# Attention with a third key stack buffer, a new order of its opening, and a low part of the keys made by VectorE in each group

## The chip, the cores and the metric

The kernel runs on one core of a Trainium2 chip. The metric is the device time of one execution in microseconds (us); lower is better.

## The reference

One layer of a perceiver: `x` is (4, 128, 512), the context is (4, 2048, 512). Three steps follow each other, each added to `x` and each behind a layer norm of it. Only the first is touched by the change:

```python
x = x + xattn(layernorm(x), ctx, ctx, w_proj, b_proj)      # 16 heads of 32, no mask
#   scores = einsum('bthd,bshd->bhts', q, k) / sqrt(32);  softmax over s;  einsum with v;  @ w_proj.T + b_proj
x = x + gated_scan_block(layernorm(x), ...)
x = x + mixture_of_experts(layernorm(x), ...)              # 8 experts, top 2, 2 shared
```

## The kernel before

**Groups.** The attention is done in 16 groups (4 batches, 4 sets of 4 heads; group j belongs to batch j // 4). A group has 128 queries, 2048 keys and 4 heads of 32 columns. Numbers are split into a high and a low half of 16 bits, so that a product of 16-bit matmuls keeps nearly the precision of 32 bits: the keys `kt` give `kh` (ScalarE, L423, two heads at a time) and `kl = kt - kh` (POOL, L590, one head at a time, 512 columns each). SyncE's queue then copies both into the *key stack* `kstk` (98 rows: high, low, high, and two rows of ones), with heads along the free dimension. Each half of the 2048 keys takes four copies of `kh` and two of `kl`. `kt`, `kh`, `kl`, `kstk` and the values `v` each have two buffers.

**Work of a group.** TensorE makes 16 blocks of 512 scores for the maxima (`max_scores`, L989), in a ring of two PSUM banks; VectorE takes the maximum of each (`take_max`, L699), and four small reductions make the shift (`shift`, L704 to L710). The shift goes in as two more rows of the queries, which are transposed again (L996). Then TensorE makes the scores a second time, transposed and shifted (`scores`, L1009, 8 steps of 256 keys), ScalarE takes the exponent (L458), POOL adds the two tiles of a step (`pair_sum`, L617), and TensorE multiplies by the values (`values`, L1024) and sums the denominators (`denominators`, L1033). VectorE inverts and divides (L716, L720) one group later.

**Order.** It is written out by hand. Group i is a loop over four parts p. The maxima of group i+1 run beside the scores of group i: blocks 4 to 7 in part 0, 8 to 12 in part 1, 13 to 15 in part 2, and then blocks 0 to 3 of group i+2 in part 3. In part 3 TensorE does blocks 0 and 1, the last two value steps of group i, and then, between the first scores of group i+1, blocks 2 and 3. Block 0 of a group waits for the first half of its key stack (`k_rep`), block 8 for the second. ScalarE splits the keys of group i+3 in parts 0 and 1, POOL makes their low parts after its fourth and sixth sum. At the start of group i SyncE's queue loads the keys of i+4 and the values of i+1, then waits for group i's scores to free the stack and fills it for i+2:

```python
        def stack(j, h):
            sp.wait_ge(split_lo, j + 1)
            if j >= 2:
                sp.wait_ge(st_done, HS * (j - 2) + HS // 2 * (h + 1))
            copies(j, h, kh, (0, 2 * HD))
            copies(j, h, kl, (HD,))
```

**Opening.** Before the loop, SyncE's queue loads batch 0 of `x`, the keys of group 0, an identity, rows of ones, the rest of `x`, and the keys of group 1. VectorE normalizes batch 0 (L730), ScalarE makes the high part of two groups' queries (L450), POOL their low part (L602), TensorE transposes them (L977) and ScalarE copies them out (`take_queries`, L435), which in its program stands behind the splitting of group 1's keys. All 16 blocks of group 0's maxima then run alone, then the shift, the first scores and the first blocks of group 1's maxima. VectorE normalizes batches 1 to 3 there.

## Time and profile before

| | |
|---|---|
| runs | 536.14 us median of 3 (534.79 to 537.72) |
| profiled execution | 541.33 us, of it 539.5 us in the span; mean granted clock 0.978 |
| TensorE busy | 471.8 us (87%) |
| VectorE busy | 398.6 us (74%) |
| ScalarE busy | 330.7 us (61%) |
| POOL busy | 293.7 us (54%) |
| maxima by VectorE (L699) | 256 of 686 ns, 163.1 us |
| 16 groups of attention | from about 20 to 294 us of the span |

A row of the timeline or of the chain begins with its start in us of the span and its length in us; "x8" is the number of instructions merged into it. In brackets stands how long the engine was idle before it, and what released it. "issue" stands where no releaser is seen in the records. PE is TensorE, PEld its weight loads, DVE is VectorE, ACT ScalarE, SPq SyncE's DMA queue.

### The profile page before, as it was taken

What the parts mean: (1) busy time and instruction counts of PE and PEld (TensorE: products, weight loads), DVE (VectorE), ACT (ScalarE), POOL (GpSimd) and SP (SyncE); (2) the same over time, 40 slices, a digit from 0 to 9 for tenths busy, and PEclk for the clock granted to TensorE, in tenths of its full rate; (3) what the DMA queues carried; (4) which work ended last, traced back from release to release, by engine and by line L of the source; (5) the groups of instructions that cost most, each with busy time, mean ns of one, the idle gap of its engine ahead of it and who ended that gap; (6) DMA issues with size and microseconds to landing.
All of it is one profiled execution on the core that took longest, in us unless ns stands there. A gap on an engine that the chain in (4) does not pass through costs nothing.

```text
span 539.5 us, 15770 instructions
## 1 busy us (share of the span) xinstructions
PE 471.8 (87%) x6731; PEld 330.4 (61%) x6731; DVE 398.6 (74%) x603; ACT 330.7 (61%) x361; POOL 293.7 (54%) x278
## 2 busy tenths in 40 slices
PE   0478998899997979999999955999999999999995
PEld 0135666666665656676667542854788787887642
DVE  2577776687775767877771799588599999999426
ACT  4245776577675766767555373367478898888320
POOL 2338898999997996999769440373001011010032
PEclk9999999999999998999999996799999999999998
DMA  8598987979979698777698721065999999998125
GB/s 266 110 267 279 254 239 185 230 226 251 258 204 261 157 258 229 230 198 180 139 391 331 293 88 68 1 197 213 421 382 398 417 416 418 416 416 348 40 77 176
DMA packets 48249, 133.94 MB, mean 248 GB/s; under 512 B 6450, under 2 KB 31282, under 8 KB 37426
## 3 DMA queue, kind: packets, MB, share of 16 engines
q1 hardware_dynamic: 44500, 120.88, 69.5%
q0 software_dynamic: 3680, 12.06, 6.1%
q8 instruction: 53, 0.87, 0.7%
q14 instruction: 16, 0.13, 0.1%
HBM read 96.74 MB, written 11.01 MB: 200 GB/s over the span
## 4 chain that ended last, share of the span: by engine, by line
PE 45%; DVE 35%; issue 8%; DMA 6%; POOL 2%; ACT 2%; SPq 1%; DVEq 0%; ACTq 0%; POOLq 0%
DVE mx L699 11%; DVE ws L773 10%; PE bank L1024 8%; PE bank L989 8%; PE bank L1033 7%; PE bank L1009 6%; DMA kt<-in_keysT 4%; DMA wst<-in_ffw 3%; DVE rden L716 2%; PE bank L1147 2%; PE bank L1148 2%; PE bank L1149 2%; DVE hf L914 2%; DVE hl L919 2%; PE bank L1090 1%
## 5 line engine op out<-in xcount | busy, mean ns | idle before, releaser
L699 DVE TENSOR_REDUCE mx<-bank 128x1 f32<-128x512 f32 x256 | 163.1, 686 | 71.2 <-PE bank L989 70.4
L458 ACT ACTIVATE pt<-bank 128x1024 f32<-128x1024 f32 x128 | 125.9, 1023 | 71.1 <-PE bank L1009 71.1
L617 POOL TENSOR_TENSOR ps<-pt 128x512 f32<-128x512 f32 x128 | 160.1, 1280 | 10.9 <-PE bank L1033 5.7
L989 PE MATMUL bank<-kstk,q 96*128 96x512 f16 x256 | 96.9, 410 | 29.2 <-issue 8.7
L773 DVE SCALAR_TENSOR_TENSOR ws<-wst,ws 128x2048 f16<-128x2048 f32 x51 | 115.5, 2287 | 2.0 <-ACT ws L502 1.8
L502 ACT ACTIVATE ws<-wst 128x2048 f16<-128x2048 f32 x48 | 90.5, 1904 | 4.6 <-DMA wst<-in_ffw 4.5
L590 POOL TENSOR_TENSOR kl<-kt,kh 128x512 f16<-128x512 f32 x62 | 70.7, 1166 | 24.9 <-ACT kh L423 24.9
L1009 PEld LDWEIGHTS bank<-q,kstk 98*128 98x128 f16 x1024 | 68.2, 100 | 23.3 <-issue 4.8
L1162 PE MATMUL bank<-xt,ws 128*128 128x128 f16 x480 | 81.2, 219 | 0.8 <-DVE hf L914 0.8
L1009 PE MATMUL bank<-q,kstk 98*128 98x128 f16 x1024 | 80.3, 223 | 1.7 <-ACT pt L458 1.0
L1164 PE MATMUL bank<-xt,ws 128*128 128x128 f16 x480 | 81.2, 219 | 0.0
L1163 PE MATMUL bank<-xt,ws 128*128 128x128 f16 x480 | 81.2, 219 | 0.0
L656 POOL DMA_DIRECT2D ys_rows<-xn x15 | 8.2, 544 | 121.0 <-ACT xn L571 121.0
L1024 PE MATMUL bank<-pt,v 128*32 128x128 f32 x2048 | 69.7, 277 | 0.6 <-issue 0.6
L989 PEld LDWEIGHTS bank<-kstk,q 96*128 96x128 f16 x256 | 22.0, 99 | 62.2 <-DVE mx L699 37.6
L1024 PEld LDWEIGHTS bank<-pt,v 128*32 128x32 f32 x2048 | 58.6, 112 | 1.7 <-issue 1.4
L1162 PEld LDWEIGHTS bank<-xt,ws 128*128 128x128 f16 x480 | 46.9, 98 | 1.2 <-DVE hf L914 1.2
L423 ACT ACTIVATE kh<-kt 128x1024 f16<-128x1024 f32 x32 | 33.4, 1053 | 22.8 <-DMA kt<-in_keysT 22.8
L1163 PEld LDWEIGHTS bank<-xt,ws 128*128 128x128 f16 x480 | 46.9, 98 | 0.0
L1164 PEld LDWEIGHTS bank<-xt,ws 128*128 128x128 f16 x480 | 46.9, 98 | 0.0
L1033 PE MATMUL bank<-ps,ones 128*32 128x128 f32 x1024 | 41.8, 281 | 0.0
L1033 PEld LDWEIGHTS bank<-ps,ones 128*32 128x32 f32 x1024 | 24.7, 110 | 15.4 <-issue 12.2
(162 smaller groups left out, 628.5 us busy)
## 6 DMA issues: line engine op xcount, KB each, us to landing
wst<-in_ffw SPq DMA_DIRECT2D x51, 1024.0 KB, 11.2
kt<-in_keysT SPq DMA_DIRECT2D x16, 1024.0 KB, 6.1
kstk<-kh SPq DMA_DIRECT2D x128, 128.0 KB, 3.4
v<-in_vals SPq DMA_DIRECT2D x16, 1024.0 KB, 9.0
kstk<-kl SPq DMA_DIRECT2D x64, 128.0 KB, 3.8
xs_rows<-biases SPq DMA_DIRECT2D x15, 256.0 KB, 3.0
x_tok<-xs_rows POOLq DMA_DIRECT2D x15, 256.0 KB, 8.4
ys_rows<-xn POOLq DMA_DIRECT2D x15, 256.0 KB, 6.6
```

What stands on the lines that cost most here:

```text
L458: act.activation(pt[:, n % 4, :, :, :].rearrange("p j a t -> p (j a t)"), bank[:, 2 * (n % 2):2 * (n % 2) + 2, :].rearrange("p j n -> p (j ...
L502: act.activation(ws[:, home_of(q), 0, m, :, :].rearrange("p c n -> p (c n)"), wst[:, q % 2, m, :, :].rearrange("p c n -> p (c n)"), ACT.Co ...
L617: pool.tensor_tensor(ps2[:, n % 4, :, :], pt[:, n % 4, 0, :, :], pt[:, n % 4, 1, :, :], ALU.add)\
L699: dve.tensor_reduce(mx[:, a, q:q + 1], bank[:, 4 + k % 2, :], AX.X, ALU.max).then_inc(m_taken, 1)
L773: dve.scalar_tensor_tensor(ws[:, home_of(q), 1, m, :, :].rearrange("p c n -> p (c n)"), wst[:, q % 2, m, :, :].rearrange("p c n -> p (c n) ...
L989: pe.matmul(bank[:, 4 + k % 2, :], q1[:, j % 2, a, :], kstk[0:KS, j % 2, a, q * 512:(q + 1) * 512], start=True, stop=True).then_inc(m_read ...
L1009: mm = pe.matmul(bank[:, 2 * (n % 2) + j, a * P:(a + 1) * P], kstk[:, i % 2, a, tile * P:(tile + 1) * P], q2[:, i % 2, a, :], start=True, ...
L1024: mm = pe.matmul(bank[a * HD:(a + 1) * HD, 6 + i % 2, 0:P], v[:, i % 2, tile, a * HD:(a + 1) * HD], pt[:, n % 4, j, a, :], start=(tile == ...
L1033: mm = pe.matmul(bank[a * HD:(a + 1) * HD, 6 + i % 2, P:2 * P], ones[:, :], ps2[:, n % 4, a, :], start=False, stop=(hs == HS - 1), skip_gr ...
L1162: pe.matmul(o, ws[:, home, 0, m, c, part], xt[:, k % 2, c, :], start=(c == 0), stop=False)
L1163: pe.matmul(o, ws[:, home, 0, m, c, part], xt[:, k % 2, C + c, :], start=False, stop=False)
L1164: mm = pe.matmul(o, ws[:, home, 1, m, c, part], xt[:, k % 2, c, :], start=False, stop=(c == C - 1))
```

## The change

The stack gets a third buffer. It lies in the second half of `wst`, the staging space of the expert weights, which is therefore loaded only after the scores of group 14. In group i the queue now fills the stack of group i+3 instead of i+2: high parts as soon as ScalarE has split, low parts behind the wait for POOL and, new, for VectorE, which makes the low part of the fourth head (`low_of_last`) at the end of part 3 of each group from 0 to 12; POOL makes three heads instead of four. The waits of the key loads follow.

In the opening, the activation tables are loaded early by two small activations; four of the copies for group 0's second half are issued by ScalarE; the queries are copied out before group 1's keys are split; group 0's maxima use six banks and are reduced two banks at a time; group 2's keys are split inside group 0 (ScalarE in parts 0 and 1, VectorE three heads in parts 1 and 2, POOL one) and group 3's there in parts 2 and 3; the first scores go before the first blocks of group 1's maxima; batches 1 to 3 are normalized in groups 1, 5 and 9, in part 1.

```diff
--- before.py
+++ after.py
@@ -141,6 +141,8 @@
     kh = temp("kh", [P, 2, HG, S // 4], F16)
     kl = temp("kl", [P, 2, HG, S // 4], F16)
     kstk = temp("kstk", [KM, 2, HG, S], F16)
+    third = wst[0:KM, 1, :, :, :].rearrange("p m c n -> p (m c n)").bitcast(F16)[:, 0:HG * S]
+    stacks = [kstk[:, 0, :, :], kstk[:, 1, :, :], third.rearrange("p (a s) -> p a s", a=HG)]
     v = temp("v", [P, 2, J, P], F32)
     pt = temp("pt", [P, 4, 2, HG, P], F32)
     ps2 = temp("ps2", [P, 4, HG, P], F32)
@@ -198,13 +200,15 @@
     consts = sem("consts_loaded")
     x_in = sem("x_loaded")
     x0_in = sem("x_first_batch_loaded")
-    id_in = sem("identity_and_ones_loaded")
+    id_in = sem("identity_loaded")
+    ones_in = sem("ones_rows_loaded")
     kt_in = [sem("kt_loaded_0"), sem("kt_loaded_1")]
     v_in = [sem("v_loaded_0"), sem("v_loaded_1")]
-    k_rep = [[sem(f"k_stacked_{q}_{h}") for h in range(2)] for q in range(2)]
+    k_rep = [[sem(f"k_stacked_{q}_{h}") for h in range(2)] for q in range(3)]
     split_hi = sem("split_hi")
     split_lo = sem("split_lo")
     lo_dve = sem("split_lo_by_vector")
+    lo_last = sem("split_lo_of_last_head")
...
@@ -318,11 +322,20 @@
     blk = block.__enter__()
 
 
+    def stack_rows(eng, j, h, src, rows):
+        for row in rows:
+            for q in (2 * h, 2 * h + 1):
+                eng.dma_start(stacks[j % 3][row:row + HD, :, q * S // 4:(q + 1) * S // 4],
+                              src[q * HD:(q + 1) * HD, j % 2, :, :]).then_inc(k_rep[j % 3][h], 16)
+
     @blk.sync
     def _(sp):
         def load_k(j):
             if j >= 2:
                 sp.wait_ge(split_lo, j - 1)
+                sp.wait_ge(lo_dve, 2 * min(j // 2, 2))
+            if j >= 5:
+                sp.wait_ge(lo_last, j - 4)
             sp.dma_start(kt[:, j % 2, :, :], t["keysT"][j]).then_inc(kt_in[j % 2], 16)
 
         def load_v(j):
@@ -331,50 +344,59 @@
             sp.dma_start(v[:, j % 2, :, :], t["vals"][j]).then_inc(v_in[j % 2], 16)
 
         def copies(j, h, src, rows):
-            for row in rows:
-                for q in (2 * h, 2 * h + 1):
-                    sp.dma_start(kstk[row:row + HD, j % 2, :, q * S // 4:(q + 1) * S // 4],
-                                 src[q * HD:(q + 1) * HD, j % 2, :, :]).then_inc(k_rep[j % 2][h], 16)
+            stack_rows(sp, j, h, src, rows)
 
         def stack(j, h):
+            sp.wait_ge(split_hi, 2 * j + 2)
+            if j >= 3:
+                sp.wait_ge(st_done, HS * (j - 3) + HS // 2 * (h + 1))
+            copies(j, h, kh, (0, 2 * HD))
             sp.wait_ge(split_lo, j + 1)
-            if j >= 2:
-                sp.wait_ge(st_done, HS * (j - 2) + HS // 2 * (h + 1))
-            copies(j, h, kh, (0, 2 * HD))
+            if j == 2:
+                sp.wait_ge(lo_dve, 4)
+            if j >= 3:
+                sp.wait_ge(lo_last, j - 2)
             copies(j, h, kl, (HD,))
 
         sp.dma_start(x[:, 0, :], t["x"][:, 0, :]).then_inc(x0_in, 16)
         load_k(0)
         sp.dma_start(idh[:, :], t["idh"]).then_inc(id_in, 16)
-        sp.dma_start(kstk[KS:KM, :, :, :], t["ones"]).then_inc(id_in, 16)
+        sp.dma_start(kstk[KS:KM, :, :, :], t["ones"]).then_inc(ones_in, 16)
+        sp.dma_start(stacks[2][KS:KM, :, :], t["ones"][:, 0, :, :]).then_inc(ones_in, 16)
+        sp.wait_ge(kt_in[0], 16)
         sp.dma_start(x[:, 1:B, :], t["x"][:, 1:B, :]).then_inc(x_in, 16)
-        load_k(1)
         sp.wait_ge(split_hi, 2)
         copies(0, 0, kh, (0, 2 * HD))
-        sp.wait_ge(lo_dve, 1)
+        sp.wait_ge(lo_dve, 2)
         sp.wait_ge(split_lo, 1)
         copies(0, 0, kl, (HD,))
-        stack(0, 1)
+        copies(0, 1, kl, (HD,))
+        load_k(1)
+        load_v(0)
         stack(1, 0)
         load_k(2)
-        load_v(0)
         stack(1, 1)
         load_k(3)
+        load_v(1)
+        stack(2, 0)
+        stack(2, 1)
         for i in range(G):
             if i + 4 < G:
                 load_k(i + 4)
-            if i + 1 < G:
+            if 0 < i < G - 1:
                 load_v(i + 1)
-            if i + 2 < G:
-                stack(i + 2, 0)
-                stack(i + 2, 1)
+            if i + 3 < G:
+                stack(i + 3, 0)
+                stack(i + 3, 1)
             if i == G - 3:
                 for dst, name in CONSTS:
                     sp.dma_start(dst, t[name]).then_inc(consts, 16)
             if i == G - 2:
-                for u in range(2):
-                    for m in range(3):
-                        sp.dma_start(wst[:, u, m, :, :], t["ffw"][2 * u, m]).then_inc(w_in[u][m], 16)
+                for m in range(3):
+                    sp.dma_start(wst[:, 0, m, :, :], t["ffw"][0, m]).then_inc(w_in[0][m], 16)
+        sp.wait_ge(st_done, HS * (G - 1))
+        for m in range(3):
+            sp.dma_start(wst[:, 1, m, :, :], t["ffw"][2, m]).then_inc(w_in[1][m], 16)
 
...
@@ -419,7 +441,7 @@
                 act.wait_ge(kt_in[j % 2], 16 * (j // 2 + 1))
                 if j >= 2:
                     for half in range(2):
-                        act.wait_ge(k_rep[j % 2][half], 16 * 6 * (j // 2))
+                        act.wait_ge(k_rep[(j - 2) % 3][half], 16 * 6 * ((j - 2) // 3 + 1))
             act.activation(kh[:, j % 2, heads, :].rearrange("p a s -> p (a s)"),
                            kt[:, j % 2, heads, :].rearrange("p a s -> p (a s)"), ACT.Copy).then_inc(split_hi, 1)
 
@@ -459,19 +481,21 @@
                            bank[:, 2 * (n % 2):2 * (n % 2) + 2, :].rearrange("p j n -> p (j n)"),
                            ACT.Exp, scale=SC).then_inc(exp_done, 1)
 
+        act.wait_ge(eps_set, 2)
+        act.activation(r1[:, 0, 0:2], eps[:, :], ACT.Sqrt)
         for h in range(2):
             split_keys(0, h)
-        act.wait_ge(eps_set, 2)
         root(ln1_var, 1, 0, 1)
+        act.wait_ge(split_hi, 2)
+        stack_rows(act, 0, 1, kh, (0, 2 * HD))
         queries_high(0)
         queries_high(1)
+        take_queries(0)
+        take_queries(1)
+        root(ln1_var, B, 1, B)
+        act.activation(r1[:, 1, 0:2], eps[:, :], ACT.Exp)
         for h in range(2):
             split_keys(1, h)
-        root(ln1_var, B, 1, B)
-        take_queries(0)
-        take_queries(1)
-        for h in range(2):
-            split_keys(2, h)
         take_shifted(0)
         exponent(0)
         exponent(1)
@@ -482,8 +506,10 @@
                     exponent(n)
                 if p == 1 and i + 2 < G:
                     take_queries(i + 2)
-                if p < 2 and i + 3 < G:
-                    split_keys(i + 3, p)
+                if i == 0 and p < 2:
+                    split_keys(2, p)
+                if p in ((2, 3) if i == 0 else (0, 1)) and i + 3 < G:
+                    split_keys(i + 3, p % 2)
                 if p == 2 and i + 1 < G:
                     take_shifted(i + 1)
                 if p == 3 and i + 3 < G:
@@ -585,29 +611,27 @@
     @blk.gpsimd
     def _(pool):
         def split_keys(j, a):
-            if a % 2 == 0:
+            if a % 2 == 0 or j in (0, 2):
                 pool.wait_ge(split_hi, 2 * j + a // 2 + 1)
             low = pool.tensor_tensor(kl[:, j % 2, a, :], kt[:, j % 2, a, :], kh[:, j % 2, a, :], ALU.subtract)
-            if a == HG - 1:
+            if a == HG - 1 or (j >= 3 and a == HG - 2):
                 low.then_inc(split_lo, 1)
 
+        pool.memset(eps[:, 0:1], EPS).then_inc(eps_set, 1)
+        pool.memset(eps[:, 1:2], EPS * 1e-8).then_inc(eps_set, 1)
         pool.memset(ones[:, :], 1.0).then_inc(ones_set, 1)
         pool.memset(one[:, :], 1.0).then_inc(one_set, 1)
         pool.memset(trih[:, 1, :], 1.0).then_inc(one_set, 1)
-        pool.memset(eps[:, 0:1], EPS).then_inc(eps_set, 1)
-        pool.memset(eps[:, 1:2], EPS * 1e-8).then_inc(eps_set, 1)
         def queries_low(j):
             q, z = queries_of(j)
             pool.wait_ge(xs_hi, j + 1)
             pool.tensor_tensor(z[:, :, 2 * HD:KS], q, z[:, :, 0:HD], ALU.subtract).then_inc(xs_lo, 1)
 
-        for a in range(2, HG):
-            split_keys(0, a)
+        split_keys(0, HG - 1)
         queries_low(0)
         queries_low(1)
-        for j in range(1, 3):
-            for a in range(HG):
-                split_keys(j, a)
+        for a in range(HG):
+            split_keys(1, a)
         queries_low(2)
 
         def pair_sum(n):
@@ -626,8 +650,10 @@
         for i in range(G):
             for hs in range(HS):
                 pair_sum(HS * i + hs)
-                if hs in (3, 5) and i + 3 < G:
-                    for a in range(hs - 3, hs - 1):
+                if i == 0 and hs == 4:
+                    split_keys(2, HG - 1)
+                if hs in ((5, 7) if i == 0 else (3, 5)) and i + 3 < G:
+                    for a in ((0, 1) if hs == (5 if i == 0 else 3) else (2,)):
                         split_keys(i + 3, a)
                 if hs == HS - 1 and i + 3 < G:
                     queries_low(i + 3)
@@ -724,29 +750,41 @@
             for b in range(b0, b1):
                 stats(x, b, ln1_var)
 
-        def first_normed(b0, b1):
-            link(dve.reciprocal(lnv[:, 2, b0:b1], lnv[:, 0, b0:b1]))
-            for b in range(b0, b1):
-                dve.tensor_scalar(xn[:, b, :], x[:, b, :], mv[:, b, 0:1], lnv[:, 2, b:b + 1], ALU.subtract,
-                                  ALU.mult).then_inc(xn_done, 1)
+        def first_normed(b):
+            dve.tensor_scalar(xn[:, b, :], x[:, b, :], mv[:, b, 0:1], lnv[:, 2, b:b + 1], ALU.subtract,
+                              ALU.mult).then_inc(xn_done, 1)
 
         dve.wait_ge(x0_in, 16)
         first_norm(0, 1)
-        dve.wait_ge(split_hi, 1)
-        dve.tensor_tensor(kl[:, 0, 0:2, :], kt[:, 0, 0:2, :], kh[:, 0, 0:2, :], ALU.subtract).then_inc(lo_dve, 1)
+        def low_parts(j, h):
+            dve.wait_ge(split_hi, 2 * j + h + 1)
+            heads = (slice(0, 2), slice(2, 3))[h]
+            dve.tensor_tensor(kl[:, j % 2, heads, :], kt[:, j % 2, heads, :], kh[:, j % 2, heads, :], ALU.subtract)\
+                .then_inc(lo_dve, 1)
+
+        def low_of_last(j):
+            dve.wait_ge(split_hi, 2 * j + 2)
+            dve.tensor_tensor(kl[:, j % 2, HG - 1, :], kt[:, j % 2, HG - 1, :], kh[:, j % 2, HG - 1, :],
+                              ALU.subtract).then_inc(lo_last, 1)
+
+        low_parts(0, 0)
+        low_parts(0, 1)
         dve.wait_ge(roots, 1)
-        first_normed(0, 1)
+        link(dve.reciprocal(lnv[:, 2, 0:1], lnv[:, 0, 0:1]))
+        first_normed(0)
         dve.wait_ge(xn_done, 1)
         dve.wait_ge(x_in, 16)
         first_norm(1, B)
-        for k in range(MB):
-            take_max(0, k)
+        for k in range(0, MB, 2):
+            a, q = block_of(k)
+            dve.wait_ge(m_ready, k + 2)
+            pair = 2 * (k // 2 % 3)
+            dve.tensor_reduce(mx[:, a, q:q + 2], bank[:, pair:pair + 2, :], AX.X, ALU.max).then_inc(m_taken, 2)
         shift(0)
         for j, k in maxima_in(-1, 3):
             take_max(j, k)
         dve.wait_ge(roots, 2)
-        first_normed(1, B)
-        dve.wait_ge(xn_done, B)
+        link(dve.reciprocal(lnv[:, 2, 1:B], lnv[:, 0, 1:B]))
 
...
@@ -763,8 +801,14 @@
                 if p == 0 and i > 0:
                     invert(i - 1)
                     divide(i - 1)
+                if p == 1 and i in (1, 5, 9):
+                    first_normed(i // C + 1)
                 if p == 2 and i + 1 < G:
                     shift(i + 1)
+                if p in (1, 2) and i == 0:
+                    low_parts(2, p - 1)
+                if p == 3 and i + 3 < G:
+                    low_of_last(i + 3)
         invert(G - 1)
         divide(G - 1)
 
@@ -983,10 +1027,13 @@
             if k == 0:
                 pe.wait_ge(q1_done, j + 1)
             if k % (2 * HG) == 0:
-                pe.wait_ge(k_rep[j % 2][k // (2 * HG)], 16 * 6 * (j // 2 + 1))
-            if j > 0 or k >= 2:
+                pe.wait_ge(k_rep[j % 3][k // (2 * HG)], 16 * 6 * (j // 3 + 1))
+            if j > 0:
                 pe.wait_ge(m_taken, MB * j + k - 1)
-            pe.matmul(bank[:, 4 + k % 2, :], q1[:, j % 2, a, :], kstk[0:KS, j % 2, a, q * 512:(q + 1) * 512],
+            elif k >= 6 and k % 2 == 0:
+                pe.wait_ge(m_taken, k - 4)
+            home = 4 + k % 2 if j > 0 else k % 6
+            pe.matmul(bank[:, home, :], q1[:, j % 2, a, :], stacks[j % 3][0:KS, a, q * 512:(q + 1) * 512],
                       start=True, stop=True).then_inc(m_ready, 1)
 
...
@@ -1007,7 +1054,7 @@
                 tile = 2 * hs + j
                 for a in range(HG):
                     mm = pe.matmul(bank[:, 2 * (n % 2) + j, a * P:(a + 1) * P],
-                                   kstk[:, i % 2, a, tile * P:(tile + 1) * P], q2[:, i % 2, a, :],
+                                   stacks[i % 3][:, a, tile * P:(tile + 1) * P], q2[:, i % 2, a, :],
                                    start=True, stop=True)
             mm.then_inc(st_done, 1)
 
@@ -1035,7 +1082,7 @@
             mm.then_inc(den_done, 1)
 
         pe.wait_ge(ones_set, 1)
-        pe.wait_ge(id_in, 32)
+        pe.wait_ge(id_in, 16)
         queries(0)
         queries(1)
         for k in range(MB):
@@ -1062,7 +1109,11 @@
             for n in done:
                 values(n)
 
-        first_products(-1, 3)
+        pe.wait_ge(ones_in, 32)
+        scores(0)
+        scores(1)
+        for j, k in maxima_in(-1, 3):
+            max_scores(j, k)
         for i in range(G):
             for p in range(3):
                 first_products(i, p)
```

## Rows read from the trace of the kernel before

**Rows 1.** Chain of waits, VectorE's reciprocals (start, length), first and last of 14.

```profile
61.69 0.88 DVE rden L716
...
270.74 0.96 DVE rden L716
```

**Rows 2.** Waits over 60 to 276 us (sum, times, longest); TensorE's timeline.

```profile
PE bank L989 <- issue: 8.7, 6, 2.5
...
104.18 0.59 PE L989 MATMUL bank<-kstk,q 96*128 96x512 f16 x2 [1.68 <-issue]
```

**Rows 3.** Timeline of VectorE, one group and the start of the next.

```profile
221.38 3.87 DVE L699 TENSOR_REDUCE mx<-bank 128x1 f32<-128x512 f32 x6 [1.15 <-PE bank L989]
...
226.16 0.29 DVE L720 TENSOR_TENSOR ao_wproj<-bank,rden 128x128 f32<-128x128 f32 x1
226.36 3.12 DVE L699 TENSOR_REDUCE mx<-bank 128x1 f32<-128x512 f32 x5
230.49 1.89 DVE L699 TENSOR_REDUCE mx<-bank 128x1 f32<-128x512 f32 x3 [1.01 <-PE bank L989]
...
236.58 1.96 DVE L699 TENSOR_REDUCE mx<-bank 128x1 f32<-128x512 f32 x3 [1.15 <-PE bank L989]
```

**Rows 4.** Timeline of VectorE in the opening, its low part of two heads.

```profile
8.54 1.23 DVE L736 TENSOR_TENSOR kl<-kt,kh 128x1024 f16<-128x1024 f32 x1 [3.04 <-ACT kh L423]
```

**Rows 5.** Timelines of POOL and ScalarE around the same group's start.

```profile
220.53 2.51 POOL L617 TENSOR_TENSOR ps<-pt 128x512 f32<-128x512 f32 x2
223.48 0.42 POOL L602 TENSOR_TENSOR xs<-xn,xs 128x128 f16<-128x128 f32 x1 [0.45 <-ACT xs L450]
...
228.78 2.29 POOL L590 TENSOR_TENSOR kl<-kt,kh 128x512 f16<-128x512 f32 x2
...
222.99 0.42 ACT L450 ACTIVATE xs<-xn 128x256 f16<-128x256 f32 x1
```

**Rows 6.** Timeline of all engines, 310 to 318 us, after the attention.

```profile
310.42 5.51 POOL L643 TENSOR_TENSOR x<-x,xn 128x512 f32<-128x512 f32 x4
...
314.91 1.17 DVE L793 TENSOR_TENSOR trih<-upper,idf 128x128 f16<-128x128 f32 x1
```

**Rows 7.** Landing of values, then of stack copies, 60 to 270; weight loads of values.

```profile
DMA to landing us min/median/max: 5.3/9.0/10.8
...
DMA to landing us min/median/max: 2.3/3.5/8.4
...
224.80 0.90 PEld L1024 LDWEIGHTS bank<-pt,v 128*32 128x32 f32 x32
```

**Rows 8.** Timeline of the opening and of group 0, in order of time.

```profile
12.29 1.24 SPq L336 DMA_DIRECT2D kstk<-kl  x2
...
21.39 1.03 PE L989 MATMUL bank<-kstk,q 96*128 96x512 f16 x2 [7.07 <-ACT q L435]
...
22.04 5.47 DVE L699 TENSOR_REDUCE mx<-bank 128x1 f32<-128x512 f32 x8 [5.79 <-PE bank L989]
...
35.95 1.28 ACT L458 ACT_TABLE_LOAD   x1
...
39.58 2.51 DVE L730 TENSOR_SCALAR xn<-x_tok,mv,lnv 128x512 f32<-128x512 f32 x3
...
50.65 1.06 ACT L423 ACTIVATE kh<-kt 128x1024 f16<-128x1024 f32 x1
...
54.07 0.18 DVE L710 TENSOR_REDUCE xs<-negm 128x4 f16<-128x8 f32 x1
...
54.97 0.60 PE L989 MATMUL bank<-kstk,q 96*128 96x512 f16 x2
...
57.60 1.94 ACT L458 ACTIVATE pt<-bank 128x1024 f32<-128x1024 f32 x2 [1.84 <-PE bank L1009]
57.82 3.87 DVE L699 TENSOR_REDUCE mx<-bank 128x1 f32<-128x512 f32 x6 [1.15 <-PE bank L989]
```

**Rows 9.** Stretches: length, busy us (count) of each engine, granted clock, DMA share, GB/s.

```profile
180.00:204.00 24.00, 20.74 (x389) 14.49 (x383) 15.51 (x31) 14.29 (x17) 23.08 (x21) 0.95 0.81 200
...
340.00:370.00 30.00, 30.00 (x226) 18.55 (x225) 21.64 (x54) 13.99 (x16) 16.87 (x11) 0.92 0.42 141
```

## The prediction, on record before the changed kernel was seen

> **What bounds the kernel now.** I read the chain of waits first, for the rhythm of the attention. The reciprocal of one group stands in it fourteen times, once per group from 1 to 14, the first at 61.69 and the last at 270.74 us [rows 1]: 209.05 us for 13 groups, 16.08 each. The VectorE timeline of one group then shows what a group costs when nothing goes wrong: from the third maximum of one group (221.38) to that of the next (236.58) are 15.2 us [rows 3]. So 13 groups hold 209.05 - 13 x 15.2 = 11.4 us of disturbance. The list of waits names most of it: before the matmuls of the maxima (L989) TensorE stood still six times, 8.7 us in all, with no engine named [rows 2]; one of them is the 1.68 us at 104.18, ahead of block 0 of the next group's maxima. There the code waits only for earlier maxima, long taken, for the queries, and for a half of the key stack, which is filled by DMAs. I read it as a stack that came late.
>
> What the reader should see in [rows 3]: VectorE is never idle from 221.38 to about 229.5 (six maxima, reciprocal, divide, five maxima), then idle for 1.01 us until 230.49. In that first half of a group VectorE sets the pace (TensorE's two-bank ring waits for it), in the second half TensorE does. Work put into the first half is paid in full; work put behind the five maxima has 1.0 us of cover. POOL is not the bound of an undisturbed group: it still waits 0.45 us for ScalarE's queries [rows 5]. It is close, though, so relieving it looks attractive and buys nothing at 15.2.
>
> **Part 1, the third stack and the new queue order.** A stack for group j+3 is now written during group j and read from the end of group j+1 on. The two low copies of its first half are issued once VectorE's last-head piece is there, about 2.1 us after the third maximum of a group; with two issues (1.25) and the slowest landing of a copy, 8.4 us [rows 7], that makes 11.8. The stack is read 57.82 - 54.97 = 2.85 us before the next third maximum [rows 8], so 12.3 after this one. Typically it has landed at 2.1 + 1.25 + 3.5 = 6.9. The late-stack wait goes: **-8.7 us**. Bounds: -8.7, and 0 if the rows' wait is DMA throughput and not the buffer.
>
> What is late next? Everything on SP's queue stands behind the wait for that last-head piece: two low copies, four high and two low ones of the second half, then the load of keys, then of values. Eight issues of 0.63 us after 2.1 are 7.1, the key load's issue makes 7.8 us. Values now land 7.8 + 9.0 = 16.8 us after the third maximum, at worst 7.8 + 10.8 = 18.6 [rows 7]. They are needed at the first value product of the next group, 224.80 - 221.38 = 3.4 us after its third maximum, so at 15.9 + 3.4 = 19.3. Cover is 2.5 us, at worst 0.7: cost 0. Keys are issued earlier and needed later.
>
> **Part 2, VectorE's piece in each group.** It stands in the program behind all four maxima that a group takes early, so between the second and third of the six maxima at 221.38 - in the half where VectorE is saturated. Price: the same operation with 1024 elements takes 1.23 us, the divide with 128 takes 0.29 [rows 3, 4]; the line between them gives 1.05 ns an element, so 0.69 us for 512, less the 0.04 by which neighbours overlap: 0.65 to 0.69. I take 0.67. Every later step of that half (the ring, the denominators, the reciprocal) moves by as much; nothing absorbs it. Between reciprocal 1 and 14 there are 12 such pieces: **+8.1 us**, bounds 0 (if the ring had slack that I do not see) and the lock below. POOL saves 2.29/2 = 1.15 us a group: 0.
>
> POOL and VectorE can get in each other's way. During POOL's four additions from 310.42 a VectorE operation with two SBUF inputs and 128 elements took 1.17 us [rows 6], four times the 0.29 of the divide, and the additions took 1.38 each. In the steady group the new piece starts about 222.75 and ends about 223.4. POOL's last two sums ended at 223.04 before; with one subtraction less they end near 221.9, and POOL is then idle until ScalarE's queries are out at 223.41 [rows 5]. So the piece falls into a gap: extra 0, bound 12 x 1.28/2 = +7.7. The Trainium skill, "SBUF — State Buffer", section "Who interferes with whom", says that a VectorE instruction with two SBUF inputs contends with a GpSimd instruction that reads SBUF, and that the one issued later waits until the other is through. By that rule the row of 1.17 is a wait for one addition, the trace agrees, and the piece would cost 8.1 us in the gap and up to 15.8 beside a sum.
>
> The three normalizations moved from the opening into groups 1, 5 and 9 take about 0.84 us each (2.51 for three, [rows 8]) and stand where 1.01 us is free, but beside a busy POOL: 0 to 0.8 each, I take 0.3: **+0.9**.
>
> **Part 3, the opening.** The second keys' load and its splitting no longer stand in front of ScalarE's copy of the first queries, which held the first maximum until 21.39 [rows 8]. Now the first half's low copies decide: two issues from 12.29 as before, the last starting at 12.9 and landing 3.5 later [rows 7]: 16.4, so 5.0 earlier. The maxima go in eight pairs of 1024 columns. The 16 single ones took 2 x 5.47 us; a pair costs one fixed part less: 0.69 = 0.15 + 0.53, so 1.22, less overlap 1.17, times 8 = 9.4 against 11.1 with the gap: 1.7. One pair must be full before the first reduction, which gives back 0.4. Together **-6.3 us**. The block of three normalizations, 2.51 us on the chain before, is gone, but the first four maxima of group 1 now stand behind the first scores instead of under the copy of the shifted queries; I set these against each other. The early activation tables save nothing: the load for the exponents lay beside the first scores. The four copies that ScalarE issues cost it 2.6 us (as SP's, about 0.65 each), under the wait for low copies: 0.
>
> Then two losses. Group 2's keys are split inside group 0, and the last low part is VectorE's, behind the shift that ended at 54.25 before (54.07 + 0.18), so at 47.95 + 0.3 to 1.5 (its first piece of 1.23 us meets the 1.0 idle, or POOL). With 0.7 for itself it ends about 49.6; the second low copy is issued at 50.2 and lands 2.9 later (between the smallest landing, 2.3, and the median, 3.5), 53.1. TensorE wants the stack at 54.97 - 6.3 = 48.7: a new wait of **+4.4 us** (3 to 6.5). And VectorE's piece for group 3 waits for ScalarE, which first does two exponents (57.60 + 1.94 = 59.54) and then 1.06 of splitting: 60.6 instead of behind the fourth maximum at 59.2 (57.82 and two maxima of 0.69). With its 0.67 that is **+2.1**, and POOL's subtraction waits for the same signal, so up to 3.3; I take 2.3. The opening sums to -6.3 + 4.4 + 2.3 = **+0.4**, from -1.5 to +4.
>
> The late load of the second weight slot waits for the scores of group 14, done before the queue gets there: 0.
>
> **The sum** against the profiled execution: 541.33 - 8.7 + 8.1 + 0.9 + 0.4 = 542.0, a change of +0.7. That execution is 5.2 us above the median of 536.14, and the clock explains most of that: 0.95 over 180 to 204 and 0.92 over 340 to 370 [rows 9] cost 1.2 + 2.4 = 3.6 us of a busy TensorE. The stack waits are thus as large in ordinary runs, and I carry the change over whole: 536.1 + 0.7 = **536.8 us**.
>
> **Rivals.** (a) *The opening's new wait is not there*: the second low part or its copies come in time. For it: the queue is empty then, and the smallest landing is 2.3. Against: the program order of VectorE. 536.8 - 4.4 = 532.4. Chance 0.20. (b) *The VectorE piece is hidden*, because TensorE runs ahead or groups stay disturbed by 0.7 anyway: 536.8 - 8.1 = 528.7. Against it: no idle in [rows 3]. Chance 0.07. (c) *The lock*, the case that ends slower: if POOL's last sums of a group do not end before the fourth maximum, the piece waits for a sum under way, 0.64 on average, in each of 12 groups: 544.5. It decides once POOL runs over 0.8 us later than in [rows 5]; POOL's place is moved by the same 0.67. Chance 0.20. (d) *Values late*, the new queue order: landings over 11.5 us or slow issues, 1 us in half of the groups: 543. Chance 0.09. (e) *The stack wait stays* because DMA throughput made it (their share is 0.81 in 180 to 204, [rows 9]): +8.7, 545.5. Chance 0.06. The forecast keeps 0.38, with a range of its own from 533.5 to 540.5.
>
> **How the numbers follow.** A measurement of this kernel can tell about 0.5% (2.7 us) from no change. Faster than that: (a), (b) and 0.02 of the forecast, 0.29. Slower: (c), (d), (e) and 0.06 of the forecast, less 0.04 where (c) or (d) is small: 0.20 + 0.09 + 0.06 + 0.06 - 0.04 = 0.37. The rest, 0.34, is no change. The range leaves out (b), (e) and the tails of the rest: 531 to 544.5.
>
> **What would show it.** In the profile after: no wait of TensorE at L989 without a releaser; the third-maximum rhythm at 15.9 instead of 15.2; a VectorE subtraction of 0.69 us right behind the fourth maximum (1.0 or more means the lock); the first matmul of the maxima near 16.4; TensorE idle some 4 us before the maxima of group 2, around 49; the first reciprocal again near 62. The prediction is wrong if the rhythm stays at 15.2, or if that idle is absent.

## The result: slower by 1.1%, and where the time went

| | us, median (range, runs) | ratio to before, 95% |
|---|---|---|
| before | 535.46 (530.42 to 537.72, 4) | |
| the changed kernel | 542.20 (540.32 to 542.91, 4) | 1.0113 (1.0065 to 1.0161) |
| the changed kernel, measured a second time | 542.05 (540.25 to 545.22, 6) | 1.0105 (1.0058 to 1.0152) |

The forecast was 536.8 (531 to 544.5), with 0.37 on slower by over 0.5%, 0.34 on no change and 0.29 on faster. The measured time lies in the range, 5.4 us above the forecast. Ratios are made from undisturbed executions, medians here and below from all of them, so the two do not always agree in the last few tenths of a per cent.

The profiled execution took 541.87 us, 540.1 in the span, at a mean granted clock of 0.974. Its engines, busy time, then the granted clock over 40 slices:

```profile
PE 472.1 (87%) x6731; PEld 330.3 (61%) x6731; DVE 409.5 (76%) x611; ACT 331.2 (61%) x362; POOL 276.1 (51%) x261
...
PEclk9999699999999999999999996899999999999998
```

POOL lost 18 us of work, VectorE gained 11. One slice, the fifth (54 to 67.5 us), stands at 0.6.

**The groups**, first by the chain of waits, then by the timelines of VectorE and POOL:

```profile
222.80 0.60 DVE kl L767
```

```profile
221.44 1.36 DVE L725 TENSOR_REDUCE mx<-bank 128x1 f32<-128x512 f32 x2 [1.15 <-PE bank L1036]
222.72 0.68 DVE L767 TENSOR_TENSOR kl<-kt,kh 128x512 f16<-128x512 f32 x1
223.31 2.53 DVE L725 TENSOR_REDUCE mx<-bank 128x1 f32<-128x512 f32 x4
...
218.92 2.53 POOL L641 TENSOR_TENSOR ps<-pt 128x512 f32<-128x512 f32 x2
223.54 0.42 POOL L628 TENSOR_TENSOR xs<-xn,xs 128x128 f16<-128x128 f32 x1 [2.10 <-ACT xs L472]
```

The piece stands where the forecast put it, between the second and third of six maxima, takes 0.68 or 0.69 us in every one of 13 groups, and falls into a gap of POOL that grew from 0.45 [rows 5] to 2.10. It is on the chain. Groups take 15.72 us, against 15.2 [rows 3]. TensorE's waits at the maxima without a releaser, 8.7 us in [rows 2], are gone from the list; over 60 to 276 us the only ones listed there are for VectorE (sum, times, longest):

```profile
PE bank L1036 <- DVE mx L725: 10.8, 29, 1.5
```

The reciprocals of groups 1 and 14 stand at 67.86 and 272.68: 204.8 us between them against 209.05 [rows 1].

**The opening** gave back more than that. In TensorE's timeline and, below, in VectorE's and POOL's:

```profile
20.79 7.96 PE L1036 MATMUL bank<-kstk,q 96*128 96x512 f16 x16 [6.64 <-DMA kstk<-kl]
...
55.61 1.01 PE L1036 MATMUL bank<-wst,q 96*128 96x512 f16 x2 [3.05 <-issue]
...
59.27 1.03 PE L1056 MATMUL bank<-q,kstk 98*128 98x128 f16 x8
```

```profile
21.91 9.14 DVE L782 TENSOR_REDUCE mx<-bank 128x2 f32<-128x1024 f32 x8 [4.78 <-PE bank L1036]
...
63.55 0.69 DVE L767 TENSOR_TENSOR kl<-kt,kh 128x512 f16<-128x512 f32 x1 [1.09 <-ACT kh L445]
...
63.59 1.66 POOL L616 TENSOR_TENSOR kl<-kt,kh 128x512 f16<-128x512 f32 x1 [6.05 <-ACT kh L445]
```

The first maximum came at 20.8, only 0.6 us earlier than before [rows 8], and waited for the low copies of the stack. The maxima end at 31.05 instead of about 33.15, a gain of 2.1. Then the new wait of 3.05 us before group 2's maxima, which start at 55.61 instead of 54.97: 0.6 late. From there to the reciprocal of group 1 are 12.25 us, against 61.69 - 54.97 = 6.72 before. VectorE and POOL wait there for ScalarE, and TensorE runs slow: its granted clock is 0.50 over 55 to 60, the lower of its two levels (1.2 and 2.4 GHz), and eight score matmuls take 1.03 us at 59.27, against 0.61 at 69.27. The stretch from 55 to 69, with the granted clock third from the end:

```profile
55.00:69.00 14.00, 11.28 (x137) 7.76 (x138) 7.05 (x11) 6.18 (x7) 7.95 (x8) 0.65 0.75 190
```

### The profile page after: what moved, and what is told of

It reads as the page before. It is cut to its first block, busy times and chain, and to the rows that moved or that the text cites. A ratio compares the mean times of both kernels' runs of the same rounds, so it can differ in the third digit from the quotient of the medians.

```text
span 540.1 us, 15811 instructions
## 1 busy us (share of the span) xinstructions
PE 472.1 (87%) x6731; PEld 330.3 (61%) x6731; DVE 409.5 (76%) x611; ACT 331.2 (61%) x362; POOL 276.1 (51%) x261
## 4 chain that ended last, share of the span: by engine, by line
PE 43%; DVE 39%; issue 8%; DMA 5%; ACT 2%; POOL 1%; SPq 1%; DVEq 0%; ACTq 0%; POOLq 0%
DVE mx L725 12%; DVE ws L817 10%; PE bank L1071 8%; PE bank L1036 7%; PE bank L1080 7%; PE bank L1056 6%; DMA wst<-in_ffw 3%; DVE rden L742 2%; PE bank L1198 2%; PE bank L1199 2%; PE bank L1200 2%; DVE hf L958 2%; DVE hl L963 1%; DVE kl L767 1%; DMA kstk<-kl 1%
## 5 line engine op out<-in xcount | busy, mean ns | idle before, releaser
L725 DVE TENSOR_REDUCE mx<-bank 128x1 f32<-128x512 f32 x240 | 153.0, 685 | 56.6 <-PE bank L1036 56.1
L480 ACT ACTIVATE pt<-bank 128x1024 f32<-128x1024 f32 x128 | 127.4, 1024 | 75.0 <-PE bank L1056 75.0
L1036 PE MATMUL bank<-kstk,q 96*128 96x512 f16 x176 | 66.6, 420 | 18.1 <-DVE mx L725 7.8
L616 POOL TENSOR_TENSOR kl<-kt,kh 128x512 f16<-128x512 f32 x45 | 53.0, 1192 | 27.6 <-ACT kh L445 27.6
L1056 PEld LDWEIGHTS bank<-q,kstk 98*128 98x128 f16 x704 | 48.1, 102 | 16.3 <-issue 5.0
L1056 PE MATMUL bank<-q,kstk 98*128 98x128 f16 x704 | 56.4, 227 | 1.7 <-ACT pt L480 1.0
L1036 PEld LDWEIGHTS bank<-kstk,q 96*128 96x128 f16 x176 | 15.2, 101 | 42.9 <-DVE mx L725 25.8
L1036 PE MATMUL bank<-wst,q 96*128 96x512 f16 x80 | 29.3, 399 | 9.5 <-DVE mx L725 4.7
```

What stands on the lines that cost most here:

```text
L480: act.activation(pt[:, n % 4, :, :, :].rearrange("p j a t -> p (j a t)"), bank[:, 2 * (n % 2):2 * (n % 2) + 2, :].rearrange("p j n -> p (j ...
L725: dve.tensor_reduce(mx[:, a, q:q + 1], bank[:, 4 + k % 2, :], AX.X, ALU.max).then_inc(m_taken, 1)
L1036: pe.matmul(bank[:, home, :], q1[:, j % 2, a, :], stacks[j % 3][0:KS, a, q * 512:(q + 1) * 512], start=True, stop=True).then_inc(m_ready, 1)
L1056: mm = pe.matmul(bank[:, 2 * (n % 2) + j, a * P:(a + 1) * P], stacks[i % 3][:, a, tile * P:(tile + 1) * P], q2[:, i % 2, a, :], start=True ...
```

## The experiments

Twelve runs were made, of ten edited kernels and of the two kernels themselves again, each beside the kernel before. All have the same landmarks: the reciprocal of group 1 closes the opening, and from it to that of group 14 are 13 groups. The runs come from three sets, in which the median of before stood at 537.34 (before_again, third_only, piece_only, pool_all), 537.78 (piece_early, group2_early, serial_copies, combined) and 536.01 (the other four); in the first measurement it was 535.46. So a median compared across sets is uncertain by about 2 us; smaller differences can be told only within a set or by the ratios. The profile is that of one execution, and can be off the median by a few us.

| kernel | reciprocal 1 | mean group | median us | ratio to before, 95% |
|---|---|---|---|---|
| before, first profile | 61.69 | 16.08 | | |
| before_again | 61.72 | 15.87 | 536.88 | 0.999 (0.9945 to 1.0035) |
| third_only | 63.07 | 15.83 | 539.99 | 1.0119 (1.008 to 1.0158) |
| piece_only | 60.22 | 19.47 | 581.66 | 1.0823 (1.0712 to 1.0933) |
| changed, first profile | 67.86 | 15.76 | 542.20 | 1.0113 (1.0065 to 1.0161) |
| after_again | 65.32 | 16.22 | 542.05 | 1.0105 (1.0058 to 1.0152) |
| piece_twice | 67.96 | 16.95 | 556.78 | 1.0399 (1.0338 to 1.0459) |
| pool_all | 62.58 | 15.51 | 536.26 | 0.9969 (0.9915 to 1.0022) |
| piece_early | 66.95 | 15.65 | 539.15 | 1.0048 (1.0005 to 1.0092) |
| group2_early | 58.97 | 16.02 | 535.29 | 0.996 (0.9925 to 0.9996) |
| serial_copies | 65.86 | 15.89 | 540.14 | 1.0051 (1.0015 to 1.0087) |
| combined | 58.07 | 15.83 | 535.76 | 0.9851 (0.9798 to 0.9905) |
| open_and_serial | 58.34 | 15.85 | 534.94 | 0.999 (0.9951 to 1.0028) |
| no_piece | 57.65 | 15.46 | 528.83 | 0.9863 (0.9816 to 0.9911) |

**before_again**: no edit.

> The kernel before, unchanged, to see what its executions near the median (535.5) look like; the one profiled first took 541.3 with 8.7 us of unattributed waits at the matmuls of the maxima and a granted clock of 0.978. Theory A (the late stacks vary from execution to execution): a profile that comes near 535 shows about 3 us of these waits and a mean group near 15.6 us. Rival (the clock makes the difference, as the prediction said): the waits are again 8 to 9 us and the clock is above 0.985.

The profiled execution took 538.27 us (536.5 in the span), 1.4 above the median of its ten. It has fewer and shorter waits, in the list of waits over 60 to 276 us:

```profile
PE bank L989 <- issue: 6.5, 5, 2.2
```

Its clock is 0.975, no higher than the 0.978 of the first profile. Neither theory's numbers fit whole (3 us was expected, the execution was not at the median), but the clock does not explain why the first one was longer, and the waits do vary. That they are stacks landing late can be followed for three of them in before's trace: the second low copies, issued at about 79.8, 97 and 160.3 us, took 7.3, 7.2 and 8.4 us to land, so until 87.1, 104.2 and 168.7; TensorE's waits ended at 87.15, 104.18 and 168.68.

**third_only**: before with the third stack alone.

```diff
-            if j >= 2:
-                sp.wait_ge(st_done, HS * (j - 2) + HS // 2 * (h + 1))
+            if j >= 3:
+                sp.wait_ge(st_done, HS * (j - 3) + HS // 2 * (h + 1))
...
+    stacks = [kstk[:, 0, :, :], kstk[:, 1, :, :], third.rearrange("p (a s) -> p a s", a=HG)]
```

> Before with the third stack buffer alone: same opening, same queue order, POOL makes all low parts; only the wait of the copies for a free stack goes back one group more. Theory A (the wait was for a free buffer): no unattributed wait at the maxima, groups of 15.2 us, 3 to 9 us faster than before, 527 to 532. Rival (the stack comes late because the DMAs have no more throughput): the waits stay and the time is that of before, 535.5.

A miss: not faster but slower, by 1.2% in the ratio and by 0.5% (2.7 us) in the medians of all executions. The copies no longer wait for a buffer, so they are issued right behind the loads of keys and values and land later, 6.9 us in the median over 60 to 270 against 3.5 [rows 7]. TensorE's waits without a releaser at the maxima fall from 6.5 us in before_again to 2.1, but others of the kind appear elsewhere, 6.2 us in all, and the groups are no shorter: 15.83 against 15.87. The row for the maxima in the list of waits, then TensorE's timeline:

```profile
PE bank L994 <- issue: 2.1, 3, 1.2
```

```profile
88.14 0.59 PE L994 MATMUL bank<-kstk,q 96*128 96x512 f16 x2 [1.25 <-issue]
...
183.24 0.63 PE L1038 MATMUL bank<-ps,ones 128*32 128x128 f32 x13
185.47 0.30 PE L1038 MATMUL bank<-ps,ones 128*32 128x128 f32 x2 [1.59 <-issue]
```

The last row is a stop in the middle of 16 matmuls, where the code has no wait; what it is stays open. So the buffer alone does not take the waits away. In pool_all, below, the buffer and the new order together do; that the reason is the earlier issue, by most of a group, is argued from the code and was not tested by itself. The first reciprocal also comes 1.35 us later than in before_again, for which no cause was sought.

**piece_only**: before with VectorE's piece alone.

```diff
+            if j >= 3:
+                sp.wait_ge(lo_last, j - 2)
...
+                if p == 3 and i + 3 < G:
+                    low_of_last(i + 3)
```

> Before with VectorE's piece of each group alone (two stacks, old opening), placed as in the changed kernel. Theory A (it stands where VectorE is saturated, 0.53 us a group in the changed kernel's profile, 12 groups between the first and the last reciprocal and one in group 0): 3 to 7 us slower, 539 to 542, less where a group waits for its stack anyway; undisturbed groups of 15.7. Rival (POOL's relief pays for it): 535.5 or less, groups of 15.2.

Both theories missed by far: 8.2% slower, groups of 19.5. The load of keys at the start of a group now waits for the piece, so that it and the load of values behind it go out late: the keys 2.3 us before the group's reciprocal, against 4.6 us before it (89.17 and 93.79) in before. The stack copies, which wait for the scores to free a stack, go out no later, 0.8 us before the reciprocal in both, but now right behind 2 MB of loads, and take longer to land. The second low copy, issued at 124.08, took 9.0 us, and TensorE's wait ended at 133.13. Over 60 to 276 us TensorE stood 29.5 us at the maxima with no releaser, eleven times. The piece is not affordable in the old order with two stacks. SP's timeline of before (keys and high copies of one group):

```profile
89.17 1.92 SPq L326 DMA_DIRECT2D kt<-in_keysT  x1
...
93.01 2.62 SPq L336 DMA_DIRECT2D kstk<-kh  x4
```

In piece_only, the timelines of SP and TensorE (reciprocal at 121.61), the low copy in the DMA issues over 124.9 to 125.4, and the list of waits:

```profile
119.32 0.33 SPq L329 DMA_DIRECT2D kt<-in_keysT  x1
...
120.83 2.56 SPq L339 DMA_DIRECT2D kstk<-kh  x4
123.43 2.06 SPq L339 DMA_DIRECT2D kstk<-kl  x2
...
133.13 0.59 PE L1001 MATMUL bank<-kstk,q 96*128 96x512 f16 x2 [2.00 <-issue]
```

```profile
kstk<-kl SPq DMA_DIRECT2D x1, 128.0 KB, 9.0
```

```profile
PE bank L1001 <- issue: 29.5, 11, 4.5
```

**pool_all**: the changed kernel, POOL makes the fourth head again.

```diff
-                if p == 3 and i + 3 < G:
-                    low_of_last(i + 3)
...
-                    for a in ((0, 1) if hs == (5 if i == 0 else 3) else (2,)):
+                    for a in ((0, 1) if hs == (5 if i == 0 else 3) else (2, 3)):
```

> The changed kernel with the fourth low part given back to POOL in groups 0 to 12; third stack and opening as changed. Theory A: groups of 15.2 without waits, 12 x 0.53 = 6.4 us less than the changed kernel and about 1 more in group 0 where VectorE waited for ScalarE: 534 to 536. Rival (POOL becomes the bound without the piece): groups of 15.5 or more, above 538.

As theory A said: ten groups in a row of 15.2 us (112.24 to 264.15 in the reciprocals), no wait without a releaser at the maxima, and a median 5.9 us under the changed kernel's, at the upper end of what was expected. Before that the groups take 17.3, 16.9 and 15.4 us, and TensorE waits for POOL's sums there (1.7 us in three waits at the denominators): POOL is behind after the opening and catches up only over three groups. VectorE's timeline at the start of group 1 shows the six maxima in one piece again:

```profile
58.79 3.87 DVE L721 TENSOR_REDUCE mx<-bank 128x1 f32<-128x512 f32 x6 [1.15 <-PE bank L1030]
62.58 0.95 DVE L738 RECIPROCAL rden<-bank 128x128 f32<-128x128 f32 x1
```

The wait before group 2's maxima is the same here, 3.01 us, and the clock over 55 to 69 is 1.00. From the start of those maxima (55.94) to the reciprocal are 6.64 us, as in before (6.72): with neither the piece nor a low clock there, nothing is lost in this stretch. In the three longer groups part of the saving is lost again, so the profiles differ by only 3.3 us between the reciprocals.

**piece_early**: the piece before the last two early maxima instead of behind them.

```diff
+                    if p == 3 and i > 0 and m == 1 and i + 3 < G:
+                        low_of_last(i + 3)
```

> The changed kernel with VectorE's piece of groups 1 to 12 moved in front of the last two of the four early maxima, into the 1.1 us in which VectorE waits for TensorE. Theory A (place decides): the groups go back from 15.7 to 15.2 us, 5 to 6 us less, 536 to 537. Rival (the lock: a piece with two SBUF inputs beside one of POOL's sums): POOL's last two sums of a group run just there (218.92 to 221.45 in the changed kernel's profile), so the piece shows 1.0 to 1.9 us instead of 0.68 and the groups stay at 15.5 to 16.0: 539 to 545.

Something of both came: seven groups of 15.2 us as theory A had it (the last of them holds no piece), the others of up to 16.9, and a median 3 us under the changed kernel's, which is in the rival's range. The intervals of the two ratios overlap, so the gain is not certain. The lock is there to be seen, VectorE's piece above, POOL's two sums below:

```profile
218.84 2.31 DVE L767 TENSOR_TENSOR kl<-kt,kh 128x512 f16<-128x512 f32 x1
...
218.09 2.51 POOL L641 TENSOR_TENSOR ps<-pt 128x512 f32<-128x512 f32 x2
```

2.31 us instead of 0.68: the piece ends at 221.15, 0.55 after POOL's second sum, so it waited for the sum under way and for the next one too. Over the groups it took between 0.68 and 2.32. The Trainium skill, "SBUF — State Buffer", section "Who interferes with whom", says that a VectorE instruction with two SBUF inputs contends with a GpSimd instruction that reads SBUF. The trace agrees, and adds that the wait can last for more than one instruction.

**group2_early**: group 2's keys split before the loop.

```diff
+        for h in range(2):
+            split_keys(2, h)
         for i in range(G):
...
-                if p in (1, 2) and i == 0:
-                    low_parts(2, p - 1)
+                if p in (0, 1) and i == 0:
+                    low_parts(2, p)
```

> The changed kernel with group 2's keys split before the loop by ScalarE, their low parts by VectorE in parts 0 and 1 and by POOL after its second sum, and group 3's high parts one part earlier. Theory A (the opening's new wait and what follows it cost the time): no wait of 3 us before group 2's maxima, no low clock behind it, VectorE's piece for group 3 without a wait; the first reciprocal moves from 67.9 to 60 to 62: 5 to 8 us less, 534 to 537. Rival (the stack is late there anyway, by DMA): the wait shrinks by less than 1 us and the time stays within 2 us of 542.2.

Theory A: the wait is gone, the clock over 55 to 69 is 1.00, the reciprocal comes at 58.97, 8.9 us earlier. The medians, of two sets, differ by 6.9 us. In the profile group 2 takes 19.3 us, 3.6 more than an undisturbed group: its values, issued at 64.91, took 11.5 us to land, until 76.4 (TensorE's timeline):

```profile
76.50 1.62 PE L1071 MATMUL bank<-pt,v 128*32 128x128 f32 x32 [1.88 <-issue]
```

**serial_copies**: group 0's copies in one queue, the first half first.

```diff
-        stack_rows(act, 0, 1, kh, (0, 2 * HD))
...
+        copies(0, 1, kh, (0, 2 * HD))
         copies(0, 1, kl, (HD,))
```

> The changed kernel with group 0's copies in one queue and in the order of before: all of the first half, then the second half, none issued by ScalarE. The first matmul of the maxima was forecast at 16.4 and came at 20.8. Theory A (the twelve copies share the DMA engines, and the first half's low ones end last): the first matmul comes at 17 to 18.5, and the maxima end 2 to 3 us earlier; the time falls by 0 to 3 us, since group 2's stack is waited for later anyway. Rival (the load of the rest of x ahead of them is what is slow): the first matmul stays at 20 to 21.

Theory A again, in TensorE's timeline:

```profile
18.35 7.96 PE L1035 MATMUL bank<-kstk,q 96*128 96x512 f16 x16 [4.63 <-DMA kstk<-kl]
...
53.62 1.01 PE L1035 MATMUL bank<-wst,q 96*128 96x512 f16 x2 [3.03 <-issue]
```

2.4 us earlier at the first maximum, 2.0 at group 2's, with the wait and the low clock (0.71 over 55 to 69) behind it as in the changed kernel. The median is 2.1 us lower, too little to be told from nothing across sets. In the changed kernel the two low copies took 5.7 and 7.4 us to land; here the second, issued at about 12.5, had landed by 18.3, in 5.8.

**combined**: these three edits together.

> The three last edits together. If they are independent: 542.2 - 5.5 - 6 - 1.5, about 529, 1 to 2 percent faster than before. If the lock keeps the piece dear, or the first reciprocal does not move below 60 us, 532 to 536.

The expectation is not shown to be met. The ratio, 0.985, would meet it, but it rests on the three shortest of six executions (528.9 to 534.0); the others took 537.5 to 539.3, at about the same granted clocks (0.971 to 0.979, against 0.974 to 0.983). The median of all six, 535.8, is 0.4% below that of before beside it, and no lower than group2_early's. Its groups, 15.83, are no shorter than with the piece in its old place: beside the sums the piece takes up to 2.3 us.

**after_again**: no edit.

> The changed kernel again, beside the next three. It took 542.2 us (ratio to before 1.011). Theory: 540 to 543 again, with the wait of 3 us before group 2's maxima and a low clock in the 14 us behind it; rival: the low clock was an accident of that execution and is absent here.

542.05, with the wait (3.03 us). The profiled execution is the longest of the six, 545.22. The clock falls less there, 1.00 over 55 to 60 and 0.88 over 55 to 69, and the reciprocal is at 65.32. The maxima of group 0 end at 32.58, only 0.6 us earlier than before. Here a second wait appears, at the first value product of group 3 (TensorE's timeline, then the DMA issues over 87 to 91 us, with KB and us to landing):

```profile
99.95 1.93 PE L1071 MATMUL bank<-pt,v 128*32 128x128 f32 x32 [1.75 <-issue]
```

```profile
v<-in_vals SPq DMA_DIRECT2D x1, 1024.0 KB, 12.2
```

These values took 12.2 us to land. The clock is 0.83 over 98 to 118, and the group takes 20.2 us instead of 15.7.

**piece_twice**: the piece made a second time, into spare space.

```diff
+            dve.tensor_tensor(wst[:, 1, 2, j % 4, :].bitcast(F16)[:, 0:S // 4], kt[:, j % 2, HG - 1, :],
+                              kh[:, j % 2, HG - 1, :], ALU.subtract)
```

> The changed kernel with VectorE's piece made a second time in each of groups 0 to 12, into spare space. Theory A (VectorE is saturated there, 0.60 us for each): groups of 16.3 instead of 15.7 and 13 x 0.6 = 7.8 us more than the changed kernel. Rival (the piece costs by delaying the stack, not by its length): no more than 1 us.

Saturation is confirmed and more: +14.7 us, groups of 16.95; a cost by delaying the stack alone would have shown as a wait at the maxima of these groups, and there is none. The first piece costs 0.53, the second 1.2 to 1.4, as it outlasts POOL's gap and delays the low part of the queries (0.74 instead of 0.42) and the sums behind it; the mean clock is lower too, 0.960 against 0.975:

```profile
217.30 0.68 DVE L767 TENSOR_TENSOR wst<-kt,kh 128x512 f16<-128x512 f32 x1
217.90 0.68 DVE L769 TENSOR_TENSOR kl<-kt,kh 128x512 f16<-128x512 f32 x1
...
218.12 0.74 POOL L628 TENSOR_TENSOR xs<-xn,xs 128x128 f16<-128x128 f32 x1 [2.21 <-ACT xs L472]
```

**open_and_serial**: group2_early and serial_copies together, the piece left where the change put it.

> The changed kernel with group 2's keys split early and group 0's copies in one queue, the piece left where the change put it. If the opening gains add: first reciprocal near 58, 9 to 10 us before the changed kernel's 67.9, groups of 15.7: 533 to 535. Rival (values of group 2 late, as once in the last kernel with the early split): 1.9 to 4 us lost at the first value products of group 2.

As expected: 534.94, first reciprocal at 58.34, undisturbed groups of 15.7. It is as fast as before (0.999).

**no_piece**: the last one with POOL making the fourth low part (the edit of pool_all).

> The last one with the fourth low part given back to POOL. Theory A (third stack, order and opening are worth their full gain without the piece): first reciprocal near 58, groups of 15.2: 527 to 530, faster than before by 1 to 2 percent and faster than the one with all three edits (535.8 median). Rival (POOL, at 15.3 us of work a group, does not catch up after the opening): mean groups above 15.5, 532 to 535.

528.83, 1.4% faster than before and 2.4% faster than the changed kernel (542.05 beside it). Against open_and_serial only the piece differs: 6.1 us, of which the profiles show 5.1 between the reciprocals and 0.7 before them. POOL did keep up, as I read it because the opening no longer leaves it behind; the groups are 15.2 but for two, of which one (waits of TensorE before value products of 1.66 us at 74.43 and 0.80 at 86.08) costs 3.0 and the other 0.5. Removing those waits too was not tried.

## What held of the forecast, what did not, and where it was lucky

The time lies in the range, and slower was the likeliest of the three outcomes. The signs named for the profile came too: groups of 15.72 (15.9 forecast), a piece of 0.68, no wait without a releaser at the maxima, a new idle before group 2's maxima. But two things were luck. The profiled execution was forecast at 542.0 and took 541.87 because errors cancel: the 13 groups came out 4.2 us shorter than before where +0.3 was forecast, and the first reciprocal 6.2 us later where +0.4 was. And of the 0.37 given to slower, nearly all was for the lock, late values and stack waits that stay; none of these is what made the change slower. The opening is, whose term was thought small.

- **The late stacks go: right in mechanism, with a wrong half.** No wait without a releaser is left at the maxima of the groups from 60 us on in any profile with the new order. In the profile nearly all of the 11.4 us of disturbance went, not 8.7. But the text gave the gain to the third stack and the order as one, and third_only shows that the buffer alone gains nothing: the copies then queue behind two loads. The bound "0 if it is DMA throughput" came nearest to that case.
- **The piece, +8.1 us: right, a little too dear.** It cost 12 x 0.53 = 6.4 us between the reciprocals. The cleanest measure is no_piece against open_and_serial, in one set and differing by the piece alone: -6.1. (pool_all's -5.9 is a mixture: 3.3 in the groups, and an opening at full clock.) The duration was forecast at 0.69 and was 0.68; neighbours overlap by 0.08, not 0.04, which leaves 0.60, and the maxima around it follow each other every 0.61 us instead of every 0.64 (four in 2.53 behind the piece, six in 3.87 before). It fell into POOL's gap, as said; rival (c) did not happen in the changed kernel, and piece_early shows its mechanism at work one place further on.
- **The moved normalizations, +0.9: 0.7.** Groups 1, 5 and 9 were longer by 0.21 to 0.23 us.
- **The opening, +0.4: this term failed.** It was +3.6 (after_again) to +6.2. The gain of 6.3 was 0.6 to 2.1 at the end of the maxima. The step that failed is the landing of the first half's low copies: it was taken as 3.5 us, the median of the steady groups, and the second copy took 7.4 (issued at 13.24, landed at 20.7). Before's own opening had shown it. There the same copy, issued at about 12.9, took 8.0 us, until 20.9, so behind the wait for the queries that ended at 21.39 stood the stack, and the 5.0 us counted for freeing the queries could give only 0.5. serial_copies shows that the second queue and its order made 2.4 us of the difference to the forecast. The DMA issues over 13.1 to 13.5 in before, then over 13.25 to 13.4 in the changed kernel:

```profile
kstk<-kl SPq DMA_DIRECT2D x1, 128.0 KB, 8.0
```

```profile
kstk<-kl SPq DMA_DIRECT2D x1, 128.0 KB, 7.4
```

- **Behind it in the opening.** The new wait, put at 4.4 (3 to 6.5), was 3.05. What stood behind it, put at 2.3, was 1.9 in after_again (65.32 - 56.72 = 8.6 against 6.72) and nothing in pool_all, without the piece; so this step was right. In the first profile it was 5.5, with the clock at 0.65 in that stretch. No step of the forecast had a fall of the clock in it.
- **Carrying the change over to the median: too simple.** The first profile's 5.2 us above the median were put down to the clock. The changed kernel's profile has the same kind of dips (0.974) and lies at its own median, and before_again has the same clock with fewer waits. So part of the 8.7 us of waits belonged to that one execution, and their removal was worth less in the others. The two profiles show 11.4 and 8.7 us of disturbance over 13 groups of 15.2. An estimate for ordinary executions: the one of 536.01 us has a span of 534.2, and less 61.7 to the first reciprocal and 268.5 to 268.8 behind the last, as in the two profiles, about 204 are left for the groups, 6 more than 13 x 15.2.
- **Rival (d), late values, 0.09:** it was priced at 1 us in half of the groups. Such waits came in one group, 2 or 3, of after_again, group2_early and no_piece each, and cost more than their own length: 4.5 us for 1.75, with the clock at 0.83 behind it.

By these sizes the sum for ordinary executions is 6.4 + 0.7 + 3.6 to 6.2, less about 6 for the waits: +5 to +7. Measured were 6.7 and, the second time, 6.0. How often the clock falls in the opening of other executions is not known. The stretch behind the last reciprocal was 1.1 to 1.5 us shorter than in before; over the other profiles it varies between 266.0 and 269.9, so this may be scatter.

## What to carry to other kernels

Before work is moved to relieve an engine, ask which engine sets the pace in the very stretch where it lands: POOL waited only 0.45 us at the start of a group and was still not the bound of an undisturbed one, and 0.68 us put into VectorE's saturated half of a group cost 0.5 us in each. A further buffer helps only if the transfers that fill it are also issued early enough and not directly behind large loads on the same queue. A start that is drawn forward moves each load's due time with it; list the due times of all of them, here group 2's stack and values, before counting the gain. And before an early wait is counted as a gain, look for what would have ended just under it: here a copy that landed 0.5 us before the wait was over.

## What the runs showed of the hardware that was not expected

- A VectorE operation with two SBUF inputs took 0.68 us alone and 2.31 us beside two POOL sums in a row; it was not let in between them.
- Stack copies of 128 KB landed in 3.5 us (median) in before's order and in 6.9 when issued right behind 2 MB of loads (third_only), single ones in 9.0 (piece_only); a load of 1 MB of values took from 5.3 to 12.2 us.
- After waits of TensorE of 3 us the granted clock fell in some executions and not in others: 0.65 and 0.88 over 55 to 69 in two of the changed kernel, 0.76 in piece_early (3.00 us), 1.00 in pool_all with the same wait of 3.01 us. With the wait gone (group2_early) or down to 1.42 and 1.09 us (open_and_serial, no_piece) that stretch stood at 1.00. What decides it was not tested.
